# A four-stage sequence kernel: its third stage reads the second's tiles of 16 sequences and carries states, its filling stands between the second's last steps, and the last weights are split behind it

## The reference, cut to what matters

```python
def layer_b(x):    # second: positions are independent; attention runs over the 16 sequences
    h = LN(x + attention_over_16_sequences(x)); e = argmax_expert(h)        # 8 experts
    return LN(h + w2[e] @ gelu(w1[e] @ h + b1[e]) + b2[e])

def layer_c(x):    # third
    xn = LN(x)*g + b
    xs, z = split(xn @ W_in)
    xs = silu(causal_conv_4_taps(xs))            # along positions
    dt = softplus(xs @ dt_w + dt_b); B = xs @ B_w; C = xs @ C_w    # B, C: 16 states
    h = 0
    for t in range(256):                         # along positions
        h = h * exp(-dt[t]*A) + (dt[t]*xs[t]) * B[t];  y[t] = sum_s h[s]*C[t][s]
    return x + ((y + xs*D_param) * silu(z)) @ W_out

def layer_d(x):    # fourth: 128 -> 512 -> 512 -> 512 -> 128 per position
    h = silu(w1@x*s1) * (w2@x*s2); h = gelu(h1@h*s3); h = gelu(h2@h*s4); return (w3@h)*s5
```

## Time and profile before

| | us |
|---|---|
| median of 3 runs | 1073.43 (1069.70 to 1073.62) |
| the profiled execution | 1073.75 |
| span of its trace | 1071.9 |
| TensorE busy | 887.4 (83%) |
| VectorE busy | 671.8 (63%) |
| ScalarE busy | 572.0 (53%) |
| GpSimd busy | 492.8 (46%) |

### The profile page before, as it was taken

The page is one execution under the profiler, slowest core; times in us unless marked ns, Lnnn a source line. Parts: engine busy times, 40 slices in busy tenths (PEclk is TensorE's granted clock), DMA queues, the critical chain, the costliest instruction groups (busy, mean ns, idle before and its releaser), DMA issues.

```text
span 1071.9 us, 21820 instructions
## 1 busy us (share of the span) xinstructions
PE 887.4 (83%) x8032; PEld 712.3 (66%) x8032; DVE 671.8 (63%) x2014; ACT 572.0 (53%) x1033; POOL 492.8 (46%) x893
## 2 busy tenths in 40 slices
PE   1777778276999999998657888998849999999995
PEld 0766667165888888877535565655537888878785
DVE  3566665366588888875329998989856155180622
ACT  1434343133667666665366897977826354362631
POOL 1366665322255455434368899999840002020111
PEclk9856565555789999999867998888959999999998
DMA  9100000110000000000020000000000000000000
GB/s 307 39 10 15 10 15 17 40 50 1 2 6 12 7 12 6 12 12 11 10 84 1 1 1 1 1 1 0 2 0 1 1 1 20 1 20 0 1 20 20
DMA packets 30707, 20.67 MB, mean 19 GB/s; under 512 B 2960, under 2 KB 28952, under 8 KB 30368
## 3 DMA queue, kind: packets, MB, share of 16 engines
q1 hardware_dynamic: 25984, 12.59, 4.1%
q10 hardware_dynamic: 4640, 6.99, 1.9%
HBM read 13.28 MB, written 6.29 MB: 18 GB/s over the span
## 4 chain that ended last, share of the span: by engine, by line
PE 57%; POOL 19%; DVE 10%; issue 6%; ACT 5%; DMA 1%; ACTq 1%; POOLq 0%; SPq 0%; DVEq 0%
PE ps L1108 12%; PE ps L1109 9%; PE ps L1110 9%; PE ps L1121 6%; PE ps L1183 6%; POOL prod L529 5%; POOL term L514 4%; PE ps L1442 3%; PE ps L1176 2%; PE ps L1127 2%; PE ps L1103 2%; POOL c_ln_rs L119 2%; DVE wall L985 2%; POOL a_ln_rs L113 1%; PE ps L1160 1%
## 5 line engine op out<-in xcount | busy, mean ns | idle before, releaser
L112 POOL TENSOR_TENSOR d_ln_ve<-d_ln_mv,eps 128x4 f32<-128x4 f32 x16 | 3.2, 202 | 238.7 <-DVE d_ln_mv L106 238.7
L1108 PE MATMUL ps<-h_h,wh_h 128*128 128x512 f32 x256 | 99.6, 389 | 0.0
L1109 PE MATMUL ps<-h_h,wh_l 128*128 128x512 f32 x256 | 99.6, 389 | 0.0
L1110 PE MATMUL ps<-h_l,wh_h 128*128 128x512 f32 x256 | 99.6, 389 | 0.0
L1183 PE MATMUL ps<-w_e,he 128*128 128x128 f32 x512 | 83.3, 300 | 5.1 <-ACT he L618 4.8
L1121 PEld LDWEIGHTS ps<-mov,hbd 32*128 32x128 f32 x2048 | 85.4, 251 | 0.0
L1121 PE MATMUL ps<-mov,hbd 32*128 32x32 f32 (+1 forms) x2048 | 83.1, 324 | 0.0
L618 ACT ACTIVATE he<-ps,pp 128x256 f32<-128x256 f32 x128 | 59.8, 472 | 43.1 <-PE ps L1110 38.1
L1183 PEld LDWEIGHTS ps<-w_e,he 128*128 128x128 f32 x512 | 73.1, 211 | 7.7 <-ACT he L618 7.0
L529 POOL TENSOR_TENSOR prod<-bcT 16x256 f32<-16x256 f32 (+7 forms) x128 | 69.0, 567 | 6.3 <-ACT bcT L738 6.3
L1086 DVE TENSOR_TENSOR d_y<-ps,w_s 128x512 f32<-128x512 f32 x8 | 5.5, 691 | 102.5 <-PE ps L1442 102.5
(11 more groups left out here) (244 smaller groups left out, 2624.0 us busy)
## 6 DMA issues: line engine op xcount, KB each, us to landing
x<-x SPq DMA_DIRECT2D x32, 128.0 KB, 1.8
x<-in_x SPq DMA_DIRECT2D x16, 128.0 KB
w_h<-in_w_h ACTq DMA_DIRECT2D x2, 1024.0 KB, 8.7
xB<-x SPq DMA_DIRECT2D x32, 64.0 KB
x<-xB SPq DMA_DIRECT2D x32, 64.0 KB
out_x<-x SPq DMA_DIRECT2D x8, 256.0 KB, 2.3
w_m<-in_w_m ACTq DMA_DIRECT2D x3, 256.0 KB, 5.3
xB<-in_w_e ACTq DMA_DIRECT2D x1, 512.0 KB
```

The source lines that it names most:

```text
L1108: pe.matmul(dst, a_h, b_h, start=start, stop=True, skip_group_check=True)
L1109: pe.matmul(dst, a_l, b_h, start=False, stop=True, skip_group_check=True)
L1110: return pe.matmul(dst, a_h, b_l, start=False, stop=True, skip_group_check=True)
```

## The change

- Stage c works on stage b's tiles in `xB` (16 positions of 16 sequences). The store to `x2`, its reload and the wait for it are gone. A tile is now two halves of 16 sequences x 8 positions; the 32 chunks stay, but are 16 chains of 2.
- The scan L1031 and its decays (L693) are replaced by four elementwise operations of 128x256 on VectorE, with the state carried from tile to tile in `hc` (L1043, L1052 to L1054 of the changed kernel). The convolution takes three columns per sequence from the tile before: ScalarE's L700, and L704 beside L702.
- A new function `overlapped` writes steps -4 to -1 of stage c behind steps 12 to 15 of stage b, and step 0 behind step 16. `products` (GpSimd) and `inputs_and_outputs` (ScalarE) of tiles 0 and 1 move to the start of steps -1 and 0.
- PSUM banks of stage c are renumbered so that banks used by b's last steps are left alone; TensorE's pair sums of tile 0 wait for b's last sum.
- The split of stage d's weights stands behind stage c, on ScalarE and GpSimd; TensorE waits for `m_low`, 4.
- The exponential of `log_A` and the sign change stand at the start of stage a.
- The output is stored in eight groups of four transfers of 64 KB.

The core of the diff (buffers, their order in memory and renamed lines left out):

```diff
+def overlapped(step_b, step_c):
+    def one(step, n):
+        step(n, n % 4, lambda k: 0 <= n + k < NB)
+    for n in range(-6, NB + 1):
+        one(step_b, n)
+        if n >= NB - 4:
+            one(step_c, n - NB)
+    for n in range(1, NB + 3):
+        one(step_c, n)
...
-        STATE, IN, DT, BC, BR, PAIRS = 0, 1, 2, 3, 4, 5
+        IN, DT, BC, BR, STATE, PAIRS = 0, 1, 2, 3, 4, 5
...
 # SyncE
             load(2, 16 * ITER, load_step(x1))
-            with sp.Fori(0, ITER) as i:
-                for l in LANES:
-                    sp.wait_ge(S["b_x"], i * 2 + l + 1)
-                    for b in range(2):
-                        sp.dma_start(by_step(x2)[...], xB[...]).then_inc(S["b_stored"], 16)
-            sp.wait_ge(S["b_stored"], 32 * NB)
-            load(1, 48 * ITER, load_seq(x2))
             with sp.Fori(0, ITER_MLP) as i:
                 for l in LANES:
                     sp.wait_ge(S["d_x"], i * 2 + l + 1)
-                    sp.dma_start(out_t[bass.ds(i * 8 + 4 * l, 4)]..., x[...]).then_inc(S["d_stored"], 16)
+                    for b in range(4):
+                        sp.dma_start(by_step(out)[bass.ds(i * 8 + 4 * l + b, 1)]..., xB[...]
+                                     ).then_inc(S["d_stored"], 16)
...
 # GpSimd
-            pipelined(pool, step_b, 6, 1, NB, 4, True)
-            pool.wait_ge(S["b_stored"], 32 * NB)
...
+            def products(n, l):
+                pool.wait_ge(S["c_bcT"], n + 1)
+                if n >= 2:
+                    pool.wait_ge(S["c_g1_ps"], n - 1)
+                for j in range(CH):
+                    last = pool.tensor_tensor(prod[l][...], bcT[l][:, 1, :, j:CH], bcT[l][:, 0, :, 0:CH - j], ALU.mult)
+                last.then_inc(S["c_prod"], 1)
             def step_c(n, q, have):
+                if n == -3:
+                    pool.wait_ge(he_ps, NE * (NB - 3))
+                    pool.memset(c_xT[0][:, 0:NB, 0:3], 0.0).then_inc(zero_ready, 1)
+                    pool.memset(hc[0][:, :, 0:NB], 0.0).then_inc(zero_ready, 1)
+                if have(1) and n <= 0:
+                    products(n + 1, o)
...
-            pipelined(pool, step_c_split, 4, 3, NB, 4, True)
+            overlapped(step_b, step_c)
+            pool.wait_ge(w_loaded["d"], W_ALL["d"])
+            for i, (hi, lo, w) in enumerate(last_weights):
+                pool.wait_ge(m_split, i + 1)
+                pool.tensor_tensor(lo, w, hi.bitcast(F32), ALU.subtract).then_inc(m_low, 1)
...
 # ScalarE
             act.wait_ge(w_loaded["a"], W_ALL["a"])
+            act.activation(expA[:, :], vec("log_A"), ACT.Exp).then_inc(expA_ready, 1)
...
                 if have(2):
                     act.wait_ge(S["c_t_ps"], n + 3)
-                    act.activation(c_xT[l][:, 3:3 + NT], ps[:, IN, 0:NT], ACT.Identity, ...)
-                if have(0):
-                    act.wait_ge(S["c_dec"], n + 1)
-                    act.activation(d0[l][:, :, 1:NCH], dec[l][...], ACT.Copy).then_inc(S["c_d0"], 1)
+                    if have(1):
+                        act.wait_ge(S["c_xT_"], n + 2)
+                        act.activation(c_xT[l][:, 0:NB, 0:3], c_xT[o][:, NB:NCH, CH:CH + 3], ACT.Copy)
+                    src = ps[:, IN, 0:NT].rearrange("p (k t s) -> p k s t", k=2, t=CH)
+                    act.activation(c_xT[l][:, :, 3:3 + CH]..., src, ACT.Identity, ...)
+                    act.activation(c_xT[l][:, NB:NCH, 0:3], src[:, 0, :, CH - 3:CH], ACT.Identity, ...)
...
+            overlapped(step_b, step_c)
+            act.wait_ge(w_loaded["d"], W_ALL["d"])
+            for hi, lo, w in last_weights:
+                act.activation(hi, w, ACT.Copy).then_inc(m_split, 1)
...
 # VectorE
                 if have(4):
-                    dve.wait_ge(x_loaded[l], 48 * ITER + 16 * ((n + 4) // 2 + 1))
+                    dve.wait_ge(S["b_x"], n + 5)
...
                 if have(0):
-                    dve.wait_ge(S["c_d0"], n + 1)
-                    dve.wait_ge(S["c_st_ps"], n + 1)
-                    dve.tensor_tensor_scan(hc[l][:, 1:1 + DS * NCH], flat3(d0[l][:, :, :]), ps[:, STATE, :], ...)
+                    if have(-1):
+                        dve.wait_ge(S["c_hs"], n)
+                    chain.link(dve.tensor_tensor(hd[:, :, :], hc[l][:, :, 0:NB], decay(0), ALU.mult))
                 if have(-1):
...
                     chain.link(dve.tensor_tensor(c_r[m][:, :, :], blocks(ps[:, DT, 0:NT]), c_xn[m][:, :, :], ALU.add))
+                if have(0):
+                    dve.wait_ge(S["c_st_ps"], n + 1)
+                    chain.link(dve.tensor_tensor(hc[l][:, :, NB:NCH], hd[:, :, :], state[:, :, 0:NB], ALU.add))
+                    chain.link(dve.tensor_tensor(hd[:, :, :], hc[l][:, :, NB:NCH], decay(1), ALU.mult))
+                    dve.tensor_tensor(hc[o][:, :, 0:NB], hd[:, :, :], state[:, :, NB:NCH], ALU.add
+                                      ).then_inc(S["c_hs"], 1)
...
 # TensorE
                     pe.wait_ge(S["c_prod"], n + 2)
+                    if n == -1:
+                        pe.wait_ge(b_sum_read, NB)
...
-            pipelined(pe, step_c, 4, 3, NB, 4, True)
+            overlapped(step_b, step_c)
             pe.wait_ge(w_loaded["d"], W_ALL["d"])
-            pe.wait_ge(m_split, 8)
+            pe.wait_ge(m_low, 4)
```

211 lines of the change are left out of this document (93 added, 118 removed).

## The result

The changed kernel takes 1082.56 us (median of 4 runs, 1081.65 to 1083.93) against 1073.48 for the kernel before in the same session: a ratio of 1.0094, 95% interval 1.0070 to 1.0119. That is slower, beyond the 0.5% that the prediction set, and 9.9 us above its 1072.7, though inside its range of 1059 to 1085. The profiled execution took 1081.65 with a span of 1079.9, 8.0 more than the span before.

A forecast was written before the change was run, and what follows sets the result against it. GpSimd was taken to set stage c's pace. The terms -1.3 - 18.6 + 5.6 + 1.4 + 9.9 + 1.9 summed to -1.1 us against the profiled 1073.75, so 1072.7 us, range 1059 to 1085.

The forecast's parts named there:

- the step of c: Steady step of stage c: new VectorE operations slow GpSimd by 0.43 us per tile, +5.6 us over 13 tiles.
- the hand-over: Between stages b and c: tile 2's products start earlier without store, reload and wait, -18.6 us (bounds -12 and -24).
- the same quarter: Stage c: GpSimd's products lose 1.28 of 5.02 us beside VectorE; the new operations were charged that share.
- The sign that I had named: Stage c: GpSimd's products mostly near 5 us, with 13 intervals averaging 14.2 us, would show the forecast.
- Rival A: Stage c: VectorE becomes pace-setter, `hc` and `c_yi` come later, 1.2 us per tile, 15.6 in all: 1082.7; chance 0.18.
- The lock rival: Stage c: two operations with both operands in SBUF block GpSimd for their whole length, 10.9 us: 1078.0; chance 0.10.
- The walk: Step-by-step timing of the new order from b's tile 14 into stage c, putting tile 2's products at 566.2.
- rival C: Between b and c: filling steps only push b's experts back, gain 12 instead of 18.6 us: 1079.3; chance 0.12.
- The late split: Between stages c and d: GpSimd's low parts of the weights delay d's first statistics, +9.9 us (+8 to +13).
- The output: End of kernel: one issue of 0.379 us becomes four of about 0.636, last transfer later, +1.9 us.
- c's tail: End of stage c: `c_r` and three linked operations replace the last scan, +1.4 us (bounds 0 and +3).
- The start: Start of stage a: an early exponential brings the 1.28 us table load forward, -1.3 us.

The follow-up runs named there:

- a_hd_psum: Changed kernel with the second operand of the state update's two products read from PSUM, not SBUF (decays left out): 1070.92 us, ratio 1.0001 to the kernel before.
- a_bc_first: Changed kernel with TensorE's B and C products of the next tile and the copy `bcT` put ahead of the transposes of `hc`: 1083.19 us.
- a_out_two: Changed kernel with two of the four transfers of each of the last two output groups issued by ScalarE's queue: 1077.47 us.

## Why the prediction was wrong

The direction was wrong: the sum gave -1.1 us where 8.0 to 9.1 were measured. Six of the seven terms in the table above had the right sign, the seventh was 0; two of them, the step of c and the hand-over, were 10 us off together.

- **What bounds c.** GpSimd did set the step before. That I kept it as the one that pays was the failed step: "so net work alone fits" of VectorE, and "If the new operations cost it the same quarter, 1.68 x 0.255 = 0.43 us per tile" of GpSimd. VectorE, at 77.59 of 86 us, was so close that 0.47 us of net work and the contention on it filled it. Then it is VectorE's time that counts, and there the two products cost 0.92 + 0.63 instead of 0.84. Measured +11.8 us instead of +5.6. The sign that I had named went against it: "products mostly near 5 us", and they are at 3.7 to 4.0. In tiles 5 to 13 the step did grow by 0.48 us, close to the 0.43, but by another road, so that is luck; what I had not priced at all are tiles 2 to 5 and 13 to 15, which ran in 13.29 and 12.43 us before. I had read 13.78 as the step of every tile. For tiles 2 to 5 `a_hd_psum` gives most of it back. For the last two it doesn't, and GpSimd waits 3.47 us for `bcT` at tile 15; `a_bc_first` has 12.80 us there, which points at the chain through `hc` and TensorE, and no run settles it.
- **Rival A** (chance 0.18) forecast VectorE as the pace-setter and 1082.7, and the median is 1082.56. The engine was right, the agreement of the number is luck. Its reason was another: that `hc` comes late and `c_yi` waits. That wait went from 3.9 us to 0.1. And its 1.2 us per tile were 0.91; what made up for it in the total were the output and the hand-over, less the early start.
- **The lock rival** had the mechanism and charged it to GpSimd (1078.0). `a_hd_psum` shows it on VectorE: two SBUF operands or one is the difference of 0.83 us per tile. Its price, 2 x 0.42 = 0.84 us per tile, was close to the 0.91 measured on average.
- **The hand-over.** The walk had `t_yo` of tile 15 18.9 us behind that of tile 14; it is 20.98 in this trace and 19.5 in others. Tile 2's products come 52.87 us behind, forecast 48.87; GpSimd waits 1.56 us there for `bcT`. "-18.6" was -14.6. By parts, in these traces, it is 9.0 for the split, 3.5 for store and reload and 2.0 for the interleaving, which I had not separated (in `a_out_two` the same code has 50.12, so 2.8 us of the 4.0 are missing in some executions only); rival C's idea that the filling steps only push b's experts back was closer than the chance of 0.12.
- **The late split.** +9.9, measured +9.8, right.
- **The output.** +1.9 counted three more issues; the four of the group before stand in the same queue. Measured +4.3; `a_out_two` takes 3.4 back.
- **c's tail**: +2.1, forecast +1.4. **The start**: 1.7 at the first tile (46.90 against 48.56), some 1.3 over all traces, forecast 1.3; the remaining 2.5 of the -4.2 are the pattern of stage a's steps, which differs between executions; whether the change has a part in it is open. **Stage d** was 1.1 shorter: TensorE's products of 128x512 fall from 0.63 to 0.39 us 2.7 us after d's first one (805.51, 808.23), and did so 5.2 us after it before (800.66, 805.88). The granted clock is 0.50 from 805 to 808 us and 0.99 from there to 820; before, it was 0.52 from 800 to 806 and 1.00 from there.

What would have told me: both engines at 90% and more of the same stretch, and intervals of 12 to 14.5 us behind the average of 13.78. Then a term has to be priced on each engine and in each part of the stage.

## What to carry to other kernels

When two engines are within a few per cent of each other in a stage, the price of an edit is its price on the engine that it lands on, contention included; the one that was on the chain before is no guide. Look at where the operands lie: a VectorE product with one operand in PSUM ran in 0.42 us beside GpSimd, with both in SBUF in up to 0.99. An average over a stage is no steady step: read its beginning, middle and end apart. Work that is moved to where an engine idles must also be out of the way of its neighbour's operands. And every queue at the end of the program is to be counted with what the step before has left in it.
